# A banded attention layer: the mixes of row m-2 directly behind the scores of row m, all turns one row later, the layer's input loaded twice

## The chip, the cores and the metric

The kernel runs on one core of a Trainium2 chip. The metric is the device time of one execution in microseconds (us). All arithmetic data is float32; matrix products of the projections are made of three products of a high and a low part each.

## The reference

Two layers work on an input `x` of 128 rows x 256 tokens x 256 channels. The change touches the second layer only, which is, for each of the 128 rows by itself:

```
x2 = group_norm(x)                        # scale and shift per channel
q, k, v = split(x2 @ w_in.T + b_in)       # 4 heads of 64
scores = q @ k.T / sqrt(64)               # |i - j| <= 16 kept, else -inf
out = softmax(scores) @ v
x = x + (out @ w_out.T + b_out)
```

Its group norm is taken over all rows, so the second layer starts when the first has ended. The first layer's result `x1T` goes through memory in between.

## The kernel before

The five queues (TensorE, ScalarE, VectorE, GpSimd and the DMA queue of SyncE) each run their own hand-written list of instructions per row, `body1(m)`. A list issues in the order in which it is written; semaphores tie the lists together. `m` is the row whose scores are made in this pass, `nxt` is m+1, `last` is m-1, `far` is m+2. A pass is a software pipeline step: it holds work of several rows.

Per row TensorE does the scores (L617, 24 matmuls in the form 64x128), the projections q, k (L477) and v (L486), the final projection y (L477, input `att`), 12 matmuls each, four "turns" and the mixes. A turn transposes one head pair's probabilities through the identity matrix into the PSUM buffer `turn` (L634 to L636). The mixes multiply the turned probabilities by v (L650, form 128x64) into `mix`. There is one buffer `turn`, so a turn waits until the copy of the one before has emptied it: ScalarE copies the turns with a = 0 (L795), VectorE those with a = 1 (L1047). q and v go to `work[0]`, k and y to `work[1]`: y waits until k has been read out (`k_done`), v until q has been (`q_done`).

The other engines, per row:

- VectorE: y plus the input (L1061), eight masked minima of the scores (L1035), the reciprocals of the row sums (L1042, function `inverse`, one per group g of two heads), turn copies (L1047), the low parts of q and k (L1052, function `low`), the low part of `att` (L1077), the rounding of the normed input of row m+2 ("cast", L1082, which waits for `g_done`), its low part (L915), v plus bias (L1088).
- ScalarE: eight exponentials (L789), the high parts of q (L806) and k (L813), of `att` (L818), turn copies (L795), the edge of v (L826, L827).
- GpSimd, in this order: four normings of prob with the reciprocals of group 0 (L415, function `norms`), the normed input of row m+2 (L426, gives `g_done`), four normings of group 1.

## Time and profile before

| | us |
|---|---|
| median of 3 runs | 3655.28 |
| lowest, highest | 3653.41, 3656.13 |
| the profiled execution | 3664.15 |
| its span, first to last instruction | 3662.3 |
| first scores of the second layer, in the trace | 2366.55 |
| TensorE busy, VectorE, ScalarE, GpSimd (of the span) | 92%, 82%, 76%, 59% |

The profile comes from one execution. Its times are counted from the start of the span. The busy shares are means over both layers; for the second layer alone they are read from a stretch in its steady part. Matmuls overlap, so the time that TensorE spends on a group is read from one start to the next start, not from the durations.

### The profile page before, as it was taken

Reading aid. Unit: us, or ns where it says so; the run is one execution under the profiler, and the core shown is the slowest. Engines: PE = TensorE matmul, PEld = TensorE weight load, DVE = VectorE, ACT = ScalarE, POOL = GpSimd, SP = SyncE. Lnnn points to the kernel's source line nnn. Section 1 sums busy time; section 2 is a strip of 40 time slices with the busy share of each in tenths; the row PEclk is TensorE's granted clock in tenths of the full one; section 3 lists DMA queues with packets and bytes.
Section 4 is the critical chain, followed back from the end, with each engine's and each line's share of the span. In section 5 each row is a group of like instructions: output and inputs, shape, how many; then the busy total and the mean of one; then the engine's idle time right before and its main releaser. Section 6 shows DMA issues by size and latency. Waiting matters only on the chain.

```text
span 3662.3 us, 122873 instructions
## 1 busy us (share of the span) xinstructions
PE 3372.3 (92%) x36747; PEld 3007.4 (82%) x36747; DVE 3002.9 (82%) x10850; ACT 2776.3 (76%) x8999; POOL 2177.9 (59%) x4107
## 2 busy tenths in 40 slices
PE   4459999999999999999999999799999999999999
PEld 1148888888888888888888888699999999999998
DVE  4458988888888888888888888688888888888887
ACT  1148888988888888888888988567667677776776
POOL 0047777777777777787777777444444444444443
PEclk7569999999999999999999999899999999999999
DMA  9921111111111111111111111011111111111111
GB/s 341 349 100 54 46 49 51 44 52 45 50 52 43 52 46 48 52 43 52 46 48 50 44 52 44 30 53 52 52 52 52 52 53 54 53 52 52 52 52 47
DMA packets 189032, 238.42 MB, mean 65 GB/s; under 512 B 11824, under 2 KB 176176, under 8 KB 184752
## 3 DMA queue, kind: packets, MB, share of 16 engines
q1 hardware_dynamic: 184368, 204.17, 17.7%
q10 hardware_dynamic: 4608, 33.56, 2.5%
q8 instruction: 29, 0.48, 0.1%
q14 instruction: 27, 0.22, 0.0%
HBM read 170.57 MB, written 67.11 MB: 65 GB/s over the span
## 4 chain that ended last, share of the span: by engine, by line
PE 58%; ACT 14%; issue 11%; DMA 6%; DVE 6%; POOL 2%; DVEq 1%; SPq 1%; ACTq 1%; POOLq 0%
PE work L477 24%; ACT prob L722 7%; PE work L486 7%; PE turn L527 5%; PE score L617 5%; PE mix L650 4%; DMA x_chunk<-xT 4%; PE mix L539 3%; PE score L505 3%; DMA x_tok<-x_nat 3%; PE turn L634 3%; ACT xnT L741 2%; ACT probT L728 2%; PE turn L635 2%; PE turn L636 2%
## 5 line engine op out<-in xcount | busy, mean ns | idle before, releaser
L364 POOL TENSOR_SCALAR prob<-prob,row_inv 128x256 f32<-128x256 f32 x2048 | 1068.0, 540 | 206.1 <-DVE row_inv L932 204.9
L722 ACT ACTIVATE prob<-prob,row_min 128x256 f32<-128x256 f32 x2048 | 1028.1, 507 | 128.3 <-DVE row_min L926 123.6
L477 PE MATMUL work<-src,w 128*128 128x256 f32 x7680 | 1067.5, 288 | 10.4 <-DVE src L915 6.7
L477 PEld LDWEIGHTS work<-src,w 128*128 128x128 f32 x7680 | 951.0, 189 | 12.3 <-DVE src L915 7.4
L415 POOL TENSOR_SCALAR prob<-prob,row_inv 128x160 f32<-128x160 f32 x1024 | 391.0, 401 | 767.4 <-DVE row_inv L1042 767.4
L926 DVE CUSTOM_DVE_ANT_0 prob<-score,neg_bias 128x256 f32<-128x256 f32 x2048 | 749.5, 417 | 17.2 <-PE score L505 10.1
L527 PE MATMUL turn<-ident,prob 128*128 128x128 f32 x3072 | 484.8, 280 | 120.0 <-ACT probT L728 101.4
L789 ACT ACTIVATE prob<-prob,row_min 128x160 f32<-128x160 f32 x1024 | 431.4, 426 | 141.7 <-DVE row_min L1035 141.6
L527 PEld LDWEIGHTS turn<-ident,prob 128*128 128x128 f32 x3072 | 336.3, 141 | 233.2 <-ACT probT L728 125.6
L477 PE MATMUL work<-att,wf 128*128 128x256 f32 x3072 | 432.1, 290 | 4.4 <-DVE att L981 3.0
L486 PE MATMUL work<-w,src 128*128 128x256 f32 x3072 | 425.8, 288 | 0.0
L722 ACT ACTIVATION_READ_ACCUMULATOR prob<-prob,row_min 128x1 f32 x2048 | 397.5, 194 | 0.0
L477 PEld LDWEIGHTS work<-att,wf 128*128 128x128 f32 x3072 | 385.0, 191 | 5.1 <-DVE att L981 3.5
L486 PEld LDWEIGHTS work<-w,src 128*128 128x128 f32 x3072 | 380.6, 189 | 0.1
L728 ACT COPY probT<-turn 128x512 f32<-128x512 f32 x512 | 297.2, 580 | 76.4 <-PE turn L527 69.8
L386 POOL TENSOR_TENSOR g_tok<-x_tok,gn_row 128x512 f32<-128x512 f32 x128 | 164.5, 1285 | 189.0 <-DMA x_tok<-x_nat 181.9
L1035 DVE CUSTOM_DVE_ANT_0 prob<-score,band 128x160 f32<-128x160 f32 x1024 | 263.3, 321 | 16.5 <-issue 2.4
L505 PE MATMUL score<-kT,nqT 32*128 32x256 f32 x6144 | 251.9, 294 | 6.1 <-DVE probT L937 3.2
L539 PE MATMUL mix<-probT,v_sb 128*32 128x256 f32 x4096 | 250.3, 385 | 0.0
L505 PEld LDWEIGHTS score<-kT,nqT 32*128 32x128 f32 x6144 | 199.7, 184 | 44.3 <-DVE probT L937 14.3
L932 DVE RECIPROCAL row_inv<-row_sum 128x4 f32<-128x4 f32 x512 | 90.2, 176 | 142.3 <-ACT prob L722 135.6
L1052 DVE SCALAR_TENSOR_TENSOR kT<-work,vec_sb,kT 128x256 fp32r<-128x256 f32 x256 | 112.1, 480 | 108.8 <-ACT kT L813 108.8
(110 smaller groups left out, 6225.7 us busy)
## 6 DMA issues: line engine op xcount, KB each, us to landing
pair_chunk<-pairT ACTq DMA_DIRECT2D x32, 1024.0 KB, 8.0
x_chunk<-xT SPq DMA_DIRECT2D x32, 1024.0 KB, 8.5
x_tok<-x_nat SPq DMA_DIRECT2D x128, 256.0 KB, 3.3
x_sb<-xT SPq DMA_DIRECT2D x128, 256.0 KB, 3.4
x1T<-y_sb SPq DMA_DIRECT2D x128, 256.0 KB, 2.2
x_sb<-x1T SPq DMA_DIRECT2D x128, 256.0 KB, 2.9
outT<-y_sb SPq DMA_DIRECT2D x128, 256.0 KB, 2.2
prob<-w_d SPq DMA_DIRECT2D x1, 1024.0 KB, 8.2
```

Of the source, the lines that this page charges most:

```text
L364: pool.tensor_scalar(prob[:, h, ib], prob[:, h, ib], row_inv[:, h, ib:ib + 1], 1.0, ALU.mult, ALU.mult).then_inc(norm_done[0], 1)
L415: pool.tensor_scalar(w, w, row_inv1[:, r.base % 2, g, a, ib:ib + 1], 1.0, ALU.mult, ALU.mult).then_inc(norm_done[1], 1)
L477: ins = pe.matmul(out[:, cb], w[:, of_w, kb, cols + cb * P:cols + (cb + 1) * P], x[:, of_x, kb], start=n == 0, stop=n == len(terms) - 1)
L486: ins = pe.matmul(out[:, tb], x[:, of_x, kb, tb * P:(tb + 1) * P], w[:, of_w, kb, cols:cols + CH], start=n == 0, stop=n == len(terms) - 1)
L505: ins = pe.matmul(score[:, h, ib], nqT[q, r.base % 2, of_q, hg, ib * P:(ib + 1) * P], kT[q, r.base % 2, of_k, hg], start=n == 0, stop=n == ...
L527: ins = pe.transpose(to[:, jb * TOK + ib * P:jb * TOK + (ib + 1) * P], prob[:, h, ib, jb * P:(jb + 1) * P], ident[:])
L539: ins = pe.matmul(mix[h * D0:(h + 1) * D0, hg], v_sb[:, r.base % 2, jb, c:c + D0], probT[:, hg, h, jb], start=jb == 0, stop=jb == TB - 1, ...
L722: act.activation(prob[:, h, ib], prob[:, h, ib], ACT.Exp, bias=row_min[:, h, ib:ib + 1], scale=-1.0, accum_out=row_sum[:, h, ib:ib + 1]).t ...
L728: act.copy(probT[:, h // HPG, h % HPG].rearrange("p b t -> p (b t)"), turn[:]).then_inc(turn_done[0][0], 1)
L789: act.activation(w, w, ACT.Exp, bias=row_min1[:, m.base % 2, g, a, ib:ib + 1], scale=-1.0, accum_out=row_sum1[:, m.base % 2, g, a, ib:ib + ...
L926: dve.tensor_tensor_reduce(prob[:, h, ib], score[:, h % HPG, ib], neg_bias[:, ib, h], 1.0, 3.0e38, ALU.add, ALU.min, row_min[:, h, ib:ib + ...
L1035: dve.tensor_tensor_reduce(prob1[:, m.base % 2, g, a, ib * WIN:(ib + 1) * WIN], score[:, 2 * g + a, ib, 0:WIN], band[:, ib], 1.0, 3.0e38, ...
```

## The change

On TensorE, the mixes of row m-2 stand directly behind the scores of row m; then come the four turns of row m-1, one ahead of q, one between q and k, one between k and v, one between v and y. Before, the pass held two turns of row m-1 and two of row m, and the mixes of row m-1 stood behind k. The lists of ScalarE and VectorE follow. On VectorE the cast of row m+2 also moves ahead of the low part of k. The pipeline is one pass longer. The input is loaded twice: once for the group norm (`x_ch`, in the space of `x_tok`) and, three rows later, once for the sum with y (`x_sb`). GpSimd's list keeps its order.

```diff
+        x_ch = x_tok[:].rearrange("p r b c -> p r (b c)").rearrange("p r (c t) -> p r c t", c=CB)
...
-        v_edge = sb("v_edge", [P, 2, CH])
+        v_edge = sb("v_edge", [P, 4, CH])
...
-            rows(1, x1_v, out_v)
+            def body1(m):
+                done, far = m + -3, m + 3
+                if far.exists:
+                    wait(sp, g_done[1], far.times(1, -1))
+                    apart(sp, sp_passed)
+                    sp.dma_start(x_ch[:, far.base % 2], x1_v[:, :, far.tokens()]).then_inc(x_ch_in[far.base % 2], 16)
+                if m.exists:
+                    wait(sp, y_done[1], m.times(CB, -3 * CB))
+                    apart(sp, sp_passed)
+                    sp.dma_start(x_sb[:, m.base % XSLOTS], x1_v[:, :, m.tokens()]).then_inc(x_in[1][m.base % XSLOTS], 16)
+                if done.exists:
+                    wait(sp, y_done[1], done.times(CB, CB))
+                    apart(sp, sp_passed)
+                    sp.dma_start(out_v[:, :, done.tokens()], y_sb[:, :, done.base % 2]).then_inc(y_out[1][done.base % 2], 16)
+            over_rows(sp, 3, 3, body1)
+            for s in range(2):
+                sp.wait_ge(y_out[1][s], 16 * ROWS // 2)
...
-                    wait(pool, x_in[1][far.base % XSLOTS], far.times(16, 16, of=XSLOTS))
+                    wait(pool, x_ch_in[far.base % 2], far.times(16, 16, of=2))
                     wait(pool, src_done[1], far.times(1, -1))
                     apart(pool, pool_passed)
                     for cb in range(CB):
-                        ins = pool.tensor_scalar(g_sb[:, far.base % 2, cb], x_sb[:, far.base % XSLOTS, cb],
+                        ins = pool.tensor_scalar(g_sb[:, far.base % 2, cb], x_ch[:, far.base % 2, cb],
...
+                done = last + -1
                 if m.exists:
                     scores(m, 0)
                     scores(m, 1)
-                if last.exists:
-                    turns(last, 1, 0)
+                if done.exists:
+                    mixes(done, 0)
+                    mixes(done, 1)
+                if last.exists:
+                    turns(last, 0, 0)
                 if nxt.exists:
                     wait(pe, src_done[1], nxt.times(1, 1))
                     wait(pe, v_done[1], m.times(1, 1))
                     project(work[:, 0], w1, 0, x).then_inc(q_ps[1], 1)
                 if last.exists:
-                    turns(last, 1, 1)
-                if nxt.exists:
-                    wait(pe, y_done[1], m.times(CB, -CB))
+                    turns(last, 0, 1)
+                if nxt.exists:
+                    wait(pe, y_done[1], m.times(CB, -2 * CB))
                     project(work[:, 1], w1, CH, x).then_inc(k_ps[1], 1)
                 if last.exists:
-                    mixes(last, 0)
-                    mixes(last, 1)
-                if m.exists:
-                    turns(m, 0, 0)
+                    turns(last, 1, 0)
                 if nxt.exists:
                     wait(pe, q_done[1], nxt.times(HP, HP))
                     project_tokens(work[:, 0], w1, 2 * CH, x).then_inc(v_ps[1], 1)
-                if m.exists:
-                    turns(m, 0, 1)
-                if last.exists:
-                    wait(pe, att_done[1], last.times(1, 1))
+                if last.exists:
+                    turns(last, 1, 1)
+                if done.exists:
+                    wait(pe, att_done[1], done.times(1, 1))
                     if nxt.exists:
                         wait(pe, k_done[1], nxt.times(HP, HP))
                     else:
-                        wait(pe, y_done[1], m.times(CB, -CB))
+                        wait(pe, y_done[1], m.times(CB, -2 * CB))
                     project(work[:, 1], wf1, 0, att).then_inc(y_ps[1], 1)
-            over_rows(pe, 1, 1, body1)
+            over_rows(pe, 1, 2, body1)
...
+                done = last + -1
                 if m.exists:
                     exps(0, 0)
-                if last.exists:
-                    turn_copy(last, 1)
+                if done.exists:
+                    wait(act, mix_ps[1], done.times(HP, HP))
+                    wait(act, y_ps[1], done.times(1, 0))
+                    act.copy(att[:, HIGH], mix[:]).then_inc(att_high[1], 1)
+                if last.exists:
+                    turn_copy(last, 0)
                 if m.exists:
                     exps(0, 1)
                 if nxt.exists:
@@ -813,21 +841,18 @@
                         act.activation(kT[:, nxt.base % 2, HIGH, hp], work[:, 1, hp], ACT.Identity,
                                        bias=vec1_sb[:, 1, hp:hp + 1]).then_inc(k_high[1], 1)
                 if last.exists:
-                    wait(act, mix_ps[1], last.times(HP, HP))
-                    wait(act, y_ps[1], last.times(1, 0))
-                    act.copy(att[:, HIGH], mix[:]).then_inc(att_high[1], 1)
-                if m.exists:
-                    turn_copy(m, 0)
+                    turn_copy(last, 1)
+                if m.exists:
                     exps(1, 1)
                 if nxt.exists:
                     wait(act, v_done[1], nxt.times(1, 1))
-                    wait(act, mix_ps[1], nxt.times(HP, -HP))
-                    act.copy(v_edge[0:HALO, nxt.base % 2], v_sb[0:HALO, nxt.base % 4, 1]).then_inc(v_edge_done, 1)
-                    act.copy(v_edge[HALO:EDGE, nxt.base % 2], v_sb[P - HALO:P, nxt.base % 4, 0]).then_inc(v_edge_done, 1)
+                    wait(act, mix_ps[1], nxt.times(HP, -3 * HP))
+                    act.copy(v_edge[0:HALO, nxt.base % 4], v_sb[0:HALO, nxt.base % 4, 1]).then_inc(v_edge_done, 1)
+                    act.copy(v_edge[HALO:EDGE, nxt.base % 4], v_sb[P - HALO:P, nxt.base % 4, 0]).then_inc(v_edge_done, 1)
             act.wait_ge(prob1_clear, 1)
-            over_rows(act, 1, 1, body1)
+            over_rows(act, 1, 2, body1)
...
-                if (last + -1).exists:
-                    done = last + -1
-                    wait(dve, y_ps[1], done.times(1, 1))
-                    wait(dve, y_out[1][done.base % 2], done.times(16, 0, of=2))
+                done, old = last + -1, last + -2
+                if old.exists:
+                    wait(dve, y_ps[1], old.times(1, 1))
+                    wait(dve, y_out[1][old.base % 2], old.times(16, 0, of=2))
+                    wait(dve, x_in[1][old.base % XSLOTS], old.times(16, 16, of=XSLOTS))
+                    apart(dve, dve_passed)
                     for ob in range(CB):
-                        dve.scalar_tensor_tensor(out=y_sb[:, ob, done.base % 2], in0=work[:, 1, ob],
-                                                 scalar=y_bias[:, ob:ob + 1], in1=x_sb[:, done.base % XSLOTS, ob],
+                        dve.scalar_tensor_tensor(out=y_sb[:, ob, old.base % 2], in0=work[:, 1, ob],
+                                                 scalar=y_bias[:, ob:ob + 1], in1=x_sb[:, old.base % XSLOTS, ob],
                                                  op0=ALU.add, op1=ALU.add).then_inc(y_done[1], 1)
                 if m.exists:
                     mins(0)
                     mins(1)
+                if done.exists:
+                    wait(dve, att_high[1], done.times(1, 1))
+                    dve.tensor_tensor(att[:, LOW], mix[:], att[:, HIGH].bitcast(F32), ALU.subtract
+                                      ).then_inc(att_done[1], 1)
+                if m.exists:
                     inverse(0)
                 if last.exists:
-                    turn_copy(last, 1)
+                    turn_copy(last, 0)
                 if nxt.exists:
                     wait(dve, q_high[1], nxt.times(HP, HP))
                     low(nqT, 0, b_q1, q_done[1])
-                    wait(dve, k_high[1], nxt.times(HP, HP))
-                    low(kT, 1, vec1_sb[:, 1], k_done[1])
-                if last.exists:
-                    wait(dve, att_high[1], last.times(1, 1))
-                    dve.tensor_tensor(att[:, LOW], mix[:], att[:, HIGH].bitcast(F32), ALU.subtract
-                                      ).then_inc(att_done[1], 1)
                 if far.exists:
                     wait(dve, g_done[1], far.times(1, 1))
                     wait(dve, v_ps[1], far.times(1, -1))
                     dve.tensor_copy(src[:, far.base % 2, HIGH], g_sb[:, far.base % 2]).then_inc(src_high[1], 1)
+                if nxt.exists:
+                    wait(dve, k_high[1], nxt.times(HP, HP))
+                    low(kT, 1, vec1_sb[:, 1], k_done[1])
+                if far.exists:
                     split_low(1, far, g_sb[:, far.base % 2])
-                if m.exists:
-                    inverse(1)
                 if nxt.exists:
                     wait(dve, v_ps[1], nxt.times(1, 1))
+                    wait(dve, mix_ps[1], nxt.times(HP, -3 * HP))
                     dve.tensor_tensor(v_sb[:, nxt.base % 4], work[:, 0], bv1_sb[:].unsqueeze(1).broadcast_to([P, TB, CH]),
                                       ALU.add).then_inc(v_done[1], 1)
-                if m.exists:
-                    turn_copy(m, 0)
-            over_rows(dve, 2, 2, body1)
+                if last.exists:
+                    turn_copy(last, 1)
+                if m.exists:
+                    inverse(1)
+            over_rows(dve, 2, 3, body1)
```

TensorE's list, one row in the steady part, before. `score<-kT,nqT` are the scores, `mix` the mixes, `turn` the turns, `work<-src` q and k, `work<-w,src` v, `work<-att` y. From the scores to the turn behind the mixes:

```order
L617 MATMUL score<-kT,nqT 128x160 x24
L634 MATMUL turn<-ident,prob 128x128
L635 MATMUL turn<-ident,prob 128x128
L636 MATMUL turn<-ident_edge,prob 64x128
L477 MATMUL work<-src,w 128x256 x12
L634 MATMUL turn<-ident,prob 128x128
L635 MATMUL turn<-ident,prob 128x128
L636 MATMUL turn<-ident_edge,prob 64x128
L477 MATMUL work<-src,w 128x256 x12
L650 MATMUL mix<-probT,v_sb 64x128 x4
L650 MATMUL mix<-probT,v_edge 64x64 x2
```

The same place in TensorE's list of the change, from the scores to k:

```order
L639 MATMUL score<-kT,nqT 128x160 x24
L672 MATMUL mix<-probT,v_sb 64x128 x4
L672 MATMUL mix<-probT,v_edge 64x64 x2
L672 MATMUL mix<-probT,v_sb 64x128 x4
L672 MATMUL mix<-probT,v_edge 64x64 x2
L656 MATMUL turn<-ident,prob 128x128
L657 MATMUL turn<-ident,prob 128x128
L658 MATMUL turn<-ident_edge,prob 64x128
L499 MATMUL work<-src,w 128x256 x12
```

The mixes moved up past two turns, q and k, and stand behind the scores with nothing between them.

VectorE's list behind the last of the minima, before:

```order
L1042 RECIPROCAL row_inv<-row_sum 128x4
L1047 COPY probT<-turn 128x320
L1052 SCALAR_TENSOR_TENSOR nqT<-work,b_q,nqT 128x256 x2
L1052 SCALAR_TENSOR_TENSOR kT<-work,vec_sb,kT 128x256 x2
L1077 TENSOR_TENSOR att<-mix,att 128x512
L1082 CAST src<-g_tok 128x512
L915 TENSOR_TENSOR src<-g_tok,src 128x512
L1042 RECIPROCAL row_inv<-row_sum 128x4
L1088 TENSOR_TENSOR v_sb<-work,bv_sb 128x512
L1047 COPY probT<-turn 128x320
```

And in the change, the same place:

```order
L1096 TENSOR_TENSOR att<-mix,att 128x512
L1067 RECIPROCAL row_inv<-row_sum 128x4
L1072 COPY probT<-turn 128x320
L1077 SCALAR_TENSOR_TENSOR nqT<-work,b_q,nqT 128x256 x2
L1108 CAST src<-g_tok 128x512
L1077 SCALAR_TENSOR_TENSOR kT<-work,vec_sb,kT 128x256 x2
L940 TENSOR_TENSOR src<-g_tok,src 128x512
L1117 TENSOR_TENSOR v_sb<-work,bv_sb 128x512
L1072 COPY probT<-turn 128x320
L1067 RECIPROCAL row_inv<-row_sum 128x4
```

The low part of `att` moved ahead of the first reciprocal, the cast ahead of the low part of k, and the second reciprocal to the end of the row.

## Rows read from the trace of the kernel before

**Rows 1.** Busy time and counts per engine, granted clock, DMA share, by stretch.

```profile
400.00:1400.00 1000.00, 940.58 (x10759) 827.23 (x10758) 887.40 (x3248) 883.83 (x2755) 786.66 (x1345) 1.00 0.16 48
2800.00:3600.00 800.00, 800.00 (x8587) 765.96 (x8586) 646.39 (x2383) 560.27 (x1990) 329.05 (x796) 1.00 0.17 52
```

**Rows 2.** Chain that ended last, 2900 to 3500 us, by line.

```profile
by line: PE work L477 42.4%; PE score L617 14.7%; PE work L486 14.4%; PE mix L650 12.6%; PE turn L634 7.3%; PE turn L635 4.4%; PE turn L636 4.3%
```

**Rows 3.** Timeline of one row of layer 2, TensorE: start us, duration us.

```profile
3008.84 1.57 PE L617 MATMUL score<-kT,nqT 64*128 64x160 f32 x24
...
3010.34 0.33 PE L634 MATMUL turn<-ident,prob 128*128 128x128 f32 x1
...
3010.64 1.66 PE L477 MATMUL work<-src,w 128*128 128x256 f32 x12
...
3012.38 1.65 PE L477 MATMUL work<-src,w 128*128 128x256 f32 x12
3013.96 0.66 PE L650 MATMUL mix<-probT,v_sb 128*64 128x128 f32 x8
...
3015.22 0.33 PE L634 MATMUL turn<-ident,prob 128*128 128x128 f32 x1
...
3015.52 1.69 PE L486 MATMUL work<-w,src 128*128 128x256 f32 x12
...
3017.29 1.68 PE L477 MATMUL work<-att,wf 128*128 128x256 f32 x12
...
3018.90 1.57 PE L617 MATMUL score<-kT,nqT 64*128 64x160 f32 x24
```

**Rows 4.** The same row on ScalarE: the steps that the change puts in one chain.

```profile
3011.54 0.43 ACT L789 ACTIVATE prob<-prob,row_min 128x160 f32<-128x160 f32 x1
...
3011.96 0.42 ACT L789 ACTIVATE prob<-prob,row_min 128x160 f32<-128x160 f32 x1
...
3014.07 0.84 ACT L813 ACTIVATE kT<-work,vec_sb 128x256 fp32r<-128x256 f32 x2
...
3015.41 0.59 ACT L818 CAST att<-mix 128x512 fp32r<-128x512 f32 x1 [0.50 <-PE mix L650]
...
3015.89 0.43 ACT L795 COPY probT<-turn 128x320 f32<-128x320 f32 x1
...
3016.21 0.44 ACT L789 ACTIVATE prob<-prob,row_min 128x160 f32<-128x160 f32 x1
```

**Rows 5.** The same row on VectorE and GpSimd.

```profile
3012.51 0.18 DVE L1042 RECIPROCAL row_inv<-row_sum 128x4 f32<-128x4 f32 x1 [0.42 <-ACT prob L789]
...
3012.89 1.53 POOL L415 TENSOR_SCALAR prob<-prob,row_inv 128x160 f32<-128x160 f32 x4 [3.43 <-DVE row_inv L1042]
...
3014.40 1.09 POOL L426 TENSOR_SCALAR g_tok<-x_sb,gn_scale,gn_shift 128x256 f32<-128x256 f32 x2
3014.94 0.88 DVE L1052 SCALAR_TENSOR_TENSOR kT<-work,vec_sb,kT 128x256 fp32r<-128x256 f32 x2 [0.83 <-ACT kT L813]
...
3016.03 0.69 DVE L1077 TENSOR_TENSOR att<-mix,att 128x512 fp32r<-128x512 f32 x1 [0.21 <-ACT att L818]
...
3016.63 0.42 DVE L1082 CAST src<-g_tok 128x512 fp32r<-128x512 f32 x1
```

**Rows 6.** Chain that ended last, start of layer 2.

```profile
2356.21 1.09 POOL g_tok L426 x2
2357.39 0.73 DVE src L1082
2358.14 0.94 DVE src L915
2359.12 5.50 PE work L477 x24
```

**Rows 7.** Work on tile `g_tok`, 2355 to 2360 us: duration ns min/median/max.

```profile
L426 POOL TENSOR_SCALAR g_tok<-x_sb,gn_scale,gn_shift x4: 553/558/723, 2356.2 to 2357.8; 128x256 f32<-128x256 f32 x4
L1082 DVE CAST src<-g_tok x1: 717/717/717, 2357.4 to 2357.4; 128x512 fp32r<-128x512 f32 x1
```

More of the change, by code:

```diff
@@ L230, in conv_preact_kernel @@
         x_tok_in = [sem(f"x_tok_in{s}") for s in range(2)]
+        x_ch_in = [sem(f"x_ch_in{s}") for s in range(2)]
         gn_scaled = sem("gn_scaled")
@@ L645, in mixes @@
                     terms = [(v_sb[:, r.base % 4, jb], slice(jb * P, (jb + 1) * P), slice(jb * P, (jb + 1) * P))
-                             for jb in range(TB)] + [(v_edge[:, r.base % 2], slice(P - HALO, P + HALO), slice(TOK, TOK + EDGE))]
+                             for jb in range(TB)] + [(v_edge[:, r.base % 4], slice(P - HALO, P + HALO), slice(TOK, TOK + EDGE))]
                     for n, (v, queries, of) in enumerate(terms):
@@ L1082, in body1 @@
                     dve.tensor_copy(src[:, far.base % 2, HIGH], g_sb[:, far.base % 2]).then_inc(src_high[1], 1)
+                if nxt.exists:
+                    wait(dve, k_high[1], nxt.times(HP, HP))
+                    low(kT, 1, vec1_sb[:, 1], k_done[1])
+                if far.exists:
                     split_low(1, far, g_sb[:, far.base % 2])
+                if nxt.exists:
+                    wait(dve, v_ps[1], nxt.times(1, 1))
+                    wait(dve, mix_ps[1], nxt.times(HP, -3 * HP))
+                    dve.tensor_tensor(v_sb[:, nxt.base % 4], work[:, 0], bv1_sb[:].unsqueeze(1).broadcast_to([P, TB, CH]),
+                                      ALU.add).then_inc(v_done[1], 1)
+                if last.exists:
+                    turn_copy(last, 1)
                 if m.exists:
                     inverse(1)
-                if nxt.exists:
-                    wait(dve, v_ps[1], nxt.times(1, 1))
-                    dve.tensor_tensor(v_sb[:, nxt.base % 4], work[:, 0], bv1_sb[:].unsqueeze(1).broadcast_to([P, TB, CH]),
-                                      ALU.add).then_inc(v_done[1], 1)
-                if m.exists:
-                    turn_copy(m, 0)
-            over_rows(dve, 2, 2, body1)
+            over_rows(dve, 2, 3, body1)
 def channels(v):
```

## The prediction

> **What bounds the kernel now.** I read the busy times by stretch first, for the second layer alone. In its steady part TensorE is busy 800 us of 800 at the full granted clock (1.00, that is 2.4 GHz), VectorE 646, ScalarE 560, GpSimd 329 [rows 1]. The chain that ended last holds nothing but TensorE there [rows 2]. So the second layer takes what TensorE needs to start its matmuls, and no other engine's lateness shows. The row that I walk through lasts from 3008.84 to 3018.90 us, 10.06 us [rows 3]. From start to start it is: scores and a turn 1.80, q and a turn 1.74, k 1.58, mixes 1.26, a turn 0.30, v and a turn 1.77, y 1.61 [rows 3].
>
> **What the change takes from TensorE.** No matmul is added or removed. What changes is which forms follow each other. A turn behind the scores costs 0.30 (1.80 less 1.50, from 3008.84 to 3010.34). A turn behind k costs less: q with its turn takes 1.74, k, the same work without a turn but with mixes behind it, 1.58, so putting a turn there adds only 0.16 [rows 3]. One turn makes just this move. I price a new row from pieces: scores 1.50, mixes 1.26, a turn 0.30, q and a turn 1.74, k and a turn 1.74 (by the row of q), v and a turn 1.77, y 1.61: 9.92 us [rows 3]. That is 0.14 less per row. The one piece with no row is scores followed by mixes. Below, it is the 1.50 of scores followed by a turn, which has a change of form in it too; above, the 0.14 comes back there, and the row stays at 10.06. I take 1.50, because mixes behind scores are one change of form, as a turn behind scores is. If nothing else waited, the row would last 9.92 to 10.06 us.
>
> The Trainium skill, page TensorEngine Tiling (Array Packing), section Key Properties, says that changing the tiling mode drains TensorE. The change saves one such switch per row (scores and mixes, each in a form of its own, now stand side by side), so by this rule alone the sum would be 0.14 a row less, and the kernel faster. The trace agrees with the rule as far as the 0.14 goes; it does not show scores and mixes side by side.
>
> **What the change makes late.** Here I follow the new lists of the other engines through one pass, t = 0 at the first matmul of the scores. The mixes start at 1.50 and all that ScalarE does for group 0 now stands behind them, because its copy of `att` is second in its list, behind only two exponentials.
>
> - Mixes start 1.50. The copy of `att` starts 1.45 after the mixes start (3013.96 to 3015.41) [rows 3, 4]: t = 2.95.
> - The turn copy behind it 0.48 later, the first exponential of the pair behind that 0.32 later (3015.41, 3015.89, 3016.21) [rows 4]: 3.75.
> - Its second exponential 0.42 later (3011.54 to 3011.96), the reciprocal of group 0 0.55 after that (to 3012.51) [rows 4, 5]: 4.72. Before, the reciprocal came at t = 3.67 (3012.51 less 3008.84).
> - GpSimd's normings start 0.38 later (3012.89), its normed input of row m+2 1.51 later (3014.40) and lasts 1.09 [rows 5]: `g_done` at 7.70.
> - The cast on VectorE follows 0.09 later (2356.21 + 1.09 to 2357.39) [rows 6]: 7.79. In the new list it stands **ahead** of the low part of k. Before, GpSimd was done at t = 6.65 and the cast came at 7.79, behind the low part of k, so nobody waited.
> - Cast 0.42, low part of k 0.88 [rows 5]; neighbours on VectorE overlap by some 0.09 (the low part of `att` at 3016.03 lasts 0.69, the cast starts 3016.63) [rows 5], I take 0.08: 9.01.
> - TensorE's y writes where k lay and waits for `k_done`. A released matmul starts 0.04 after its producer's end (2358.14 + 0.94 to 2359.12) [rows 6]: y starts at 9.05 instead of 9.92 less 1.61, 8.31. A wait of 0.74 per row.
> - y to the next scores 1.61 [rows 3]: the row lasts 10.66 us.
>
> Without the cast in its way the low part of k would be in time: k starts at 1.50 + 1.26 + 0.30 + 1.74 = 4.80, ScalarE reads it 1.69 later (3012.38 to 3014.07), 0.84 long, then 0.03 and 0.88 (3014.94) [rows 3 to 5]: 8.24, and y could start at 8.28. So the cast is what decides, by its wait for GpSimd. q by the same steps: it starts at 3.06, its low part is done at 6.50, and v, which waits for it, may start at 6.54. That is without a margin, but a short wait there changes nothing at y, which starts 0.74 later anyway.
>
> Behind the waiting cast on VectorE stand the low parts of k and of the input, v plus bias, a turn copy and the second reciprocal. TensorE waits for `k_done` only: the rest is needed in the next pass. GpSimd's next normings start after the second reciprocal, about t = 10.7, and end 1.53 later, at 1.6 of the next pass; the first turn needs them at 2.76. All these have room. GpSimd cannot run ahead: in its list the normed input of row m+2 stands behind the normings of group 0 of row m, and these behind the reciprocal.
>
> The second loading adds 256 KB per row. The DMA engines are busy 0.17 of the time [rows 1] with two transfers of that size a row, so 0.25 with three. The load for row m+3 is issued when the normed input of row m+1 is done, two passes before GpSimd reads it. Cost nothing; a load that took a whole row more would still be in time. The zeroing of a `v_edge` of twice the size is one memset, once: nothing. One pass more at the end: mixes and y of the last row, 1.26 + 1.61, about 3 us [rows 3]; the first rows, which wait for nothing yet, give about 1 back.
>
> **Sum.** 10.66 less 10.06 is 0.60 a row. Of 128 rows I count 124 as steady: 74 us, and 2 for the ends: 76 us. The profiled execution, 3664.15 (span 3662.3), would become 3740. It lies 8.9 above the median of the runs shown, which I take for the difference between executions; on the median, 3655.28, the sum gives 3731 us.
>
> **Bounds.** Smaller: no gap between GpSimd and the cast and none before y (less 0.13 a row): plus 60, 3715. Larger: the 0.14 between scores and mixes comes back. It delays the whole chain, since mixes start later: plus 17, 3748. A release of TensorE as slow as that of GpSimd (0.38 less the reciprocal's 0.18, so 0.20 in place of 0.04) adds 20 [rows 5]: 3751. The likeliest case by itself has the range 3715 to 3755.
>
> A further cost is seen at the start of the layer: there the cast took 0.72 us and not 0.42, while GpSimd was still at its second pair on `g_tok` [rows 5, 7]. The Trainium skill, page SBUF — State Buffer, section SBUF: two separate sides, has VectorE and GpSimd share a pair of ports that one of them locks for a whole instruction. I don't add this 0.30: in the new steady row GpSimd has nothing to do between 7.70 and the second reciprocal, and the cast lies in that gap.
>
> **The rivals.**
>
> - **Faster: the cast is not late.** The place is GpSimd's `g_done`. If the cast started before t = 7.0, the low part of k would start when ScalarE has done its part (7.36), y would not wait, and the row would last 9.92: 0.14 x 125 less, plus 3 at the end, about 3641. For it speaks that GpSimd is busy less than half of the steady time [rows 1]; against it that its list is in order, and that my chain has to be 0.8 us shorter. It decides at a cast start of about 7.2 (y at 8.45, the row at 10.06). The rule of the Trainium skill's page on tiling, named above, is on this side. Chance 0.07. A stall of part of the size, 0.1 to 0.4 a row, gives 3670 to 3705: chance 0.05. That the stall and the gain cancel within 0.2% (7.3 us): 0.02.
> - **Much slower: a second wait joins.** VectorE has 8.1 us of work per row (646 in 800 us) [rows 1] and now waits 1.3 us at the cast; of 10.66 little is left for its other waits. Should the row's first minima slip until the copy of `att` on ScalarE comes late, or the cast hit GpSimd's work (0.30, above), I price it at 0.30: a row of 10.96, plus 114, about 3769. Chance 0.09.
> - **The granted clock falls** because TensorE now waits 7% of each row. In the first layer it idles 59 us of 1000, and the clock is 1.00 [rows 1]. Chance 0.02, price over 100 us.
>
> The likeliest case has the rest, 0.75. The range that holds the time 8 times in 10 takes it whole and reaches a little into both neighbours: 3708 to 3762. What can be told from no change is about 0.2%, 7 us. Faster 0.07, same 0.02, slower 0.91.
>
> **What the profile of the changed kernel would show.** TensorE no longer busy without gap: a wait of 0.6 to 0.9 us per row at y, released by VectorE's low part of k, and VectorE waiting some 1.3 us per row (6.50 to 7.79) at the cast for GpSimd's `g_tok`. The reciprocal of group 0 at 4.7 after the scores. From mixes to the turn behind them 1.26 as before, from scores to mixes 1.50, from k to v 1.74. The chain that ended last with ScalarE, GpSimd and VectorE in it. Granted clock 1.00. The prediction is wrong if the cast starts before 7 us in the row, if the copy of `att` is not what ScalarE's exponentials wait behind, or if rows last 9.9 us.

## The result

| | before | the change |
|---|---|---|
| median, 4 runs each | 3654.35 us | 3742.34 us |
| lowest to highest | 3650.78 to 3656.13 | 3732.01 to 3744.29 |
| ratio, 95% interval | | 1.0229 [1.0212, 1.0246] |
| span of the profiled execution | 3662.3 us | 3741.6 us |

The change makes the kernel 2.3% slower by the ratio of the runs; the medians alone are 88 us apart, 2.4%, which the interval of the ratio still holds. In the two profiled executions the second layer, from its first scores to the end, takes 85.1 us more (3741.6 - 2360.7 against 3662.3 - 2366.5 us). The first layer was 5.8 us shorter in the profile of the change; its code is the same.

The loss lies in the steady rows. Busy time by stretch, as in [rows 1] (TensorE, weight loads, VectorE, ScalarE, GpSimd, granted clock, DMA share, GB/s):

```profile
2800.00:3600.00 800.00, 760.45 (x8043) 717.72 (x8041) 595.55 (x2231) 531.56 (x1867) 308.70 (x746) 1.00 0.23 73
```

TensorE is busy 760 us of 800 and starts 8043 matmuls instead of 8587, at the same clock. Nothing runs slower; something waits. The waits of the change, 2500 to 3600 us (total us, times, longest):

```profile
...
DVE src L1108 <- POOL g_tok L448: 129.1, 103, 1.3
ACT prob L812 <- DVE row_min L1060: 121.5, 102, 1.3
PEld work L499 <- issue: 78.9, 103, 0.9
PE work L499 <- DVE kT L1077: 54.3, 103, 0.6
```

Two of them stand in no row of before: TensorE waits once a row (103 times for 103 rows) at y for the low part of k (DVE kT), and VectorE waits once a row at the cast for GpSimd. (The matmul row counts 0.5 us per row and the weight load ahead of it 0.77: the end of the matmul before is modelled. From start to start, which needs no ends, it comes out below.) The chain that ended last, 2900 to 3500 us, by line, which in [rows 2] was TensorE alone:

```profile
by line: PE work L499 15.6%; PE score L639 14.0%; issue 13.5%; PE mix L672 11.9%; POOL prob L437 10.5%; POOL g_tok L448 10.2%; ACT prob L812 8.9%; DVE kT L1077 5.2%; DVE src L1108 4.0%; DVE row_inv L1067 1.8%; ACTq L90 1.1%; ACT probT L818 
```

It now runs through all four engines. One row of it in the timeline of the change (start us, duration us), which answers to [rows 3 to 5]:

```profile
3010.14 1.57 PE L639 MATMUL score<-kT,nqT 64*128 64x160 f32 x24
...
3011.64 0.66 PE L672 MATMUL mix<-probT,v_sb 128*64 128x128 f32 x8
...
3013.09 0.59 ACT L826 CAST att<-mix 128x512 fp32r<-128x512 f32 x1 [0.51 <-PE mix L672]
...
3013.57 0.43 ACT L818 COPY probT<-turn 128x320 f32<-128x320 f32 x1
...
3013.89 0.44 ACT L812 ACTIVATE prob<-prob,row_min 128x160 f32<-128x160 f32 x1
...
3014.31 0.43 ACT L812 ACTIVATE prob<-prob,row_min 128x160 f32<-128x160 f32 x1
...
3014.86 0.18 DVE L1067 RECIPROCAL row_inv<-row_sum 128x4 f32<-128x4 f32 x1 [0.46 <-ACT prob L812]
...
3015.24 1.53 POOL L437 TENSOR_SCALAR prob<-prob,row_inv 128x160 f32<-128x160 f32 x4 [3.43 <-DVE row_inv L1067]
...
3016.76 1.09 POOL L448 TENSOR_SCALAR g_tok<-x_tok,gn_scale,gn_shift 128x256 f32<-128x256 f32 x2
...
3017.88 0.43 DVE L1108 CAST src<-g_tok 128x512 fp32r<-128x512 f32 x1 [1.24 <-POOL g_tok L448]
...
3018.23 0.87 DVE L1077 SCALAR_TENSOR_TENSOR kT<-work,vec_sb,kT 128x256 fp32r<-128x256 f32 x2
3018.25 0.27 PE L656 MATMUL turn<-ident,prob 128*128 128x128 f32 x1
...
3019.24 1.68 PE L499 MATMUL work<-att,wf 128*128 128x256 f32 x12 [0.51 <-DVE kT L1077]
```

The next scores start at 3020.85, so the row lasts 10.71 us against 10.06. Read it from the end: y starts 0.14 after the low part of k, which starts 0.35 after the cast, which starts 0.03 after GpSimd's normed input, and so on up to the mixes at 1.50 of the row. The longest gap in it between the end of one step and the start of the next is 0.20, from the reciprocal to GpSimd. The wait at y can be read from the starts alone: from the last turn to y it is 0.99 us here (3018.25 to 3019.24), and 0.24 before, where y (at 3017.29 [rows 3]) waited for nothing:

```profile
3017.05 0.27 PE L634 MATMUL turn<-ident,prob 128*128 128x128 f32 x1
```

So TensorE waits 0.75 us per row there.

### The profile page after: what moved, and what is told of

It is laid out like the page before. It is cut to its first block, busy times and chain, and to the rows that moved or that the text cites. A ratio compares the mean times of both kernels' runs of the same rounds, so it can differ in the third digit from the quotient of the medians.

```text
span 3741.6 us, 123927 instructions
## 1 busy us (share of the span) xinstructions
PE 3387.1 (91%) x36747; PEld 3005.8 (80%) x36747; DVE 2983.6 (80%) x10850; ACT 2786.7 (74%) x8999; POOL 2178.9 (58%) x4107
## 4 chain that ended last, share of the span: by engine, by line
PE 39%; ACT 17%; issue 15%; DVE 9%; POOL 9%; DMA 6%; DVEq 1%; ACTq 1%; SPq 1%; POOLq 0%
PE work L499 15%; ACT prob L745 7%; PE turn L549 5%; PE score L639 5%; PE mix L672 4%; POOL prob L437 4%; POOL g_tok L448 4%; DMA x_chunk<-xT 3%; ACT prob L812 3%; PE mix L561 3%; PE score L527 3%; DMA x_tok<-x_nat 2%; DVE kT L1077 2%; PE work L508 2%; ACT xnT L764 2%
## 5 line engine op out<-in xcount | busy, mean ns | idle before, releaser
L851 ACT COPY v_edge<-v_sb 32x256 f32<-32x256 f32 x128 | 52.0, 406 | 222.6 <-DVE v_sb L1117 222.6
```

## The experiments

Theory A is the prediction's: the cast stands ahead of the low part of k, so y waits for GpSimd; and GpSimd is late because the first reciprocal of the row stands behind the copy of `att`, which needs the mixes. Rivals: the length of VectorE's list (B), the place of the copy of `att` doesn't matter (C), the doubled load (D), the move of the cast by itself (E). F and G are rivals on GpSimd: that its idle time hides added work, and that it stays in the chain by another way. The runs e9 to e12 are on a side finding, the delay between the low part of k and y (H: two waits on one matmul cost it; I: another reason).

All runs were timed beside the kernel before on the same chip. The chips differ (the medians of before lie between 3652 and 3668 us), so the ratios are to be compared, not the times. The column "scores" is the time from the first to the last scores matmul of layer 2 in the run's own profile, less that of before. It leaves out the first layer and what follows the last scores.

| run | ratio, 95% interval | scores, us |
|---|---|---|
| the change | 1.0229 [1.0212, 1.0246] | +80.6 |
| cast behind k (e1) | 0.9987 [0.9978, 0.9996] | -11.3 |
| exponentials first (e2) | 1.0122 [1.0106, 1.0139] | +38.1 |
| normed input first (e3) | 0.9983 [0.9973, 0.9992] | -12.1 |
| before, two loads (e4) | 0.9995 [0.9987, 1.0004] | +0.1 |
| before, cast ahead (e5) | 1.0028 [1.0017, 1.0038] | +10.5 |
| GpSimd longer (e6) | 1.0420 [1.0399, 1.0442] | +148.2 |
| cast behind, GpSimd longer (e7) | 0.9995 [0.9984, 1.0005] | -11.0 |
| exponentials and reciprocal first (e8) | 0.9988 [0.9979, 0.9997] | -9.8 |
| y with one wait (e9) | 1.0226 [1.0213, 1.0239] | +70.1 |
| input first, one wait (e10) | 0.9965 [0.9952, 0.9978] | -15.1 |
| the change again (e11) | 1.0239 [1.0225, 1.0253] | +80.1 |
| one wait again (e12) | 1.0211 [1.0197, 1.0225] | +69.3 |

The rows behind that column, of the scores on TensorE, for before, the change and e1 (count, duration ns min/median/max, first and last start):

```profile
L617 PE MATMUL score<-kT,nqT x3072: 267/272/343, 2366.5 to 3645.1; 64*128 64x160 f32 x192
```

```profile
L639 PE MATMUL score<-kT,nqT x3072: 267/272/343, 2360.7 to 3719.9; 64*128 64x160 f32 x192
```

```profile
L639 PE MATMUL score<-kT,nqT x3072: 267/272/343, 2367.2 to 3634.5; 64*128 64x160 f32 x192
```

**The cast behind the low part of k (e1).**

```diff
+                if nxt.exists:
+                    wait(dve, k_high[1], nxt.times(HP, HP))
+                    low(kT, 1, vec1_sb[:, 1], k_done[1])
                 if far.exists:
                     wait(dve, g_done[1], far.times(1, 1))
                     wait(dve, v_ps[1], far.times(1, -1))
                     dve.tensor_copy(src[:, far.base % 2, HIGH], g_sb[:, far.base % 2]).then_inc(src_high[1], 1)
-                if nxt.exists:
-                    wait(dve, k_high[1], nxt.times(HP, HP))
-                    low(kT, 1, vec1_sb[:, 1], k_done[1])
```

> The changed kernel with one move on VectorE: the cast of row m+2 stands behind the low part of k again, as it did before the change. Theory A (y waits for k_done, because the cast, which waits for GpSimd's normed input, stands ahead of the low part of k): y waits no more, the row goes from 10.72 to 9.92 to 9.96 us, and the time from 3742 by some 95 us to 3647 (3638 to 3655). Rival B (the later reciprocal and VectorE's fuller list make the row long whatever stands ahead of k): most of the 0.65 us per row stays, the time is above 3700.

The ratio is 0.9987: this one place in VectorE's list is worth the whole loss, and the kernel is then slightly faster than before (0.1%; the interval ends at 0.9996). Theory B falls, since the list is as long as in the change. The waits of e1, 2600 to 3500 us:

```profile
POOL prob L437 <- DVE row_inv L1067: 529.3, 180, 3.0
...
DVE kT L1077 <- ACT kT L841: 78.9, 91, 0.9
```

VectorE waits for k itself again, not for GpSimd, and no wait of TensorE is in the list. The rows are 9.97 us on average (1267.3 less 1.3, the time from the first to the last scores matmul of one row, over 127), not quite the 9.92 of the sum. This mean is lowered by the first two rows, while the pipeline fills; in the steady part a row lasts 9.99. And y is not quite free: it still starts 0.14 us after the low part of k ends (3009.75 + 0.88 to 3010.77), as in every row of that stretch:

```profile
3009.75 0.88 DVE L1077 SCALAR_TENSOR_TENSOR kT<-work,vec_sb,kT 128x256 fp32r<-128x256 f32 x2 [0.89 <-ACT kT L841]
...
3010.77 1.67 PE L499 MATMUL work<-att,wf 128*128 128x256 f32 x12
```

The first reciprocal is as late here as in the change (4.72 of the row); it does no harm.

**The second pair of exponentials ahead of the copy of `att` on ScalarE (e2).** The exponentials `exps(0, 1)` change places with the copy of `att` and the turn copy behind it; nothing else moves.

```diff
                 if m.exists:
                     exps(0, 0)
+                if m.exists:
+                    exps(0, 1)
...
                 if last.exists:
                     turn_copy(last, 0)
-                if m.exists:
-                    exps(0, 1)
```

> The changed kernel with one move on ScalarE: the copy of att and the turn copy behind it stand behind the second pair of exponentials of group 0, so that the reciprocal needs neither the mixes nor these copies. The cast stays ahead of the low part of k. Theory A with its chain (mixes, copy of att, turn copy, exponentials, reciprocal, normings, normed input, cast): the reciprocal comes at about 3.7 us of the row instead of 4.7, GpSimd is done at about 6.7, the cast waits 0.3 us or less, the row lasts 9.92 to 10.0, the time is 3640 to 3657. Rival C (the copy of att in front of the exponentials is not what makes the chain late): 3730 to 3745.

A miss: 1.0122, rows of 10.36, about half of the loss is left. The timeline of one row of e2 shows the link that was left out:

```profile
3017.45 1.57 PE L639 MATMUL score<-kT,nqT 64*128 64x160 f32 x24
...
3020.26 0.41 ACT L812 ACTIVATE prob<-prob,row_min 128x160 f32<-128x160 f32 x1
...
3020.67 0.56 ACT L828 CAST att<-mix 128x512 fp32r<-128x512 f32 x1
...
3021.27 0.69 DVE L1096 TENSOR_TENSOR att<-mix,att 128x512 fp32r<-128x512 f32 x1 [0.56 <-ACT att L828]
...
3021.88 0.17 DVE L1067 RECIPROCAL row_inv<-row_sum 128x4 f32<-128x4 f32 x1
```

The exponentials now come first, and the last one starts at 2.81 of the row. But the reciprocal stands behind the low part of `att` on VectorE, which needs ScalarE's copy of `att`, which needs the mixes. So it came at 4.43 instead of 4.72. There are two links from the mixes to the reciprocal, one on each engine; while the first held, the second, in VectorE's list, was hidden behind it.

**Both links cut (e8).** As e2, and on VectorE:

```diff
+                if m.exists:
+                    inverse(0)
                 if done.exists:
                     wait(dve, att_high[1], done.times(1, 1))
...
-                if m.exists:
-                    inverse(0)
```

> The changed kernel with the second pair of exponentials ahead of the copy of att on ScalarE, as in the run that fell short (rows of 10.33), and in addition the first reciprocal ahead of the low part of att on VectorE. The cast stays ahead of the low part of k. In the run before, the exponentials were done at 3.3 of the row, but the reciprocal stood behind the low part of att, which waits for the copy of att, and came at 4.4. Theory A, with this second link: the reciprocal comes at 3.4, GpSimd is done at 6.35, the cast waits for nothing, the row lasts 9.95 to 10.0, the time is 0.997 to 1.000 of before. If rows stay above 10.2, the chain has a link that I don't know.

0.9988, with the cast still ahead of the low part of k. In a row of e8 whose scores start at 3014.03, the reciprocal comes at 3.29 and the cast does not wait for GpSimd, whose normed input ends at 3020.31:

```profile
3017.20 0.56 ACT L828 CAST att<-mix 128x512 fp32r<-128x512 f32 x1
3017.32 0.18 DVE L1067 RECIPROCAL row_inv<-row_sum 128x4 f32<-128x4 f32 x1
3017.79 0.69 DVE L1098 TENSOR_TENSOR att<-mix,att 128x512 fp32r<-128x512 f32 x1 [0.29 <-ACT att L828]
3019.22 1.09 POOL L448 TENSOR_SCALAR g_tok<-x_tok,gn_scale,gn_shift 128x256 f32<-128x256 f32 x2
...
3020.45 0.42 DVE L1108 CAST src<-g_tok 128x512 fp32r<-128x512 f32 x1
```

**The normed input first on GpSimd (e3).** The third place at which the chain can be cut: its step for row m+2 ahead of `norms(m, 0)` instead of behind it.

```diff
-                if m.exists:
-                    norms(m, 0)
                 if far.exists:
...
                     ins.then_inc(g_done[1], 1)
+                if m.exists:
+                    norms(m, 0)
```

> The changed kernel with one move on GpSimd: the normed input of row m+2 stands ahead of the normings of group 0 instead of behind them, so it does not need the reciprocal. Theory A: the cast finds its input ready and does not wait, the row lasts 9.92 to 9.97, the time is 3640 to 3657. Rival B (length of VectorE's list): above 3700. A rival in between (the loads come too late for an earlier normed input, or the normings, now 1.1 us later, hold up the turns): 3660 to 3700, with a wait at the turns or at GpSimd for the load.

0.9983. The loads were in time, the normings too: no wait of GpSimd for a load and none of TensorE at a turn stands in its waits, 2600 to 3500 us. Three different cuts (e1 on VectorE, e8 on ScalarE and VectorE, e3 on GpSimd) each give back the whole loss, so all of them lay in one chain. That is what theory A says, and no rival does.

**The kernel before with every row loaded twice (e4).** The second copy goes to a buffer that nobody reads.

```diff
...
+                    if n == 1 and far.exists:
+                        wait(sp, x_two_in[far.base % 2], far.times(16, 0, of=2))
+                        apart(sp, sp_passed)
+                        sp.dma_start(x_two[:, far.base % 2], of[:, :, far.tokens()]).then_inc(x_two_in[far.base % 2], 16)
...
```

> The kernel before, with every row of the second layer's input loaded a second time into a buffer that nobody reads. It prices the double load of the change by itself. Theory A: nothing, within 0.2% of 3654. Rival D (a part of the change's loss is traffic: 256 KB more per row): 10 us or more above before, with slower matmuls or later stores in the trace.

0.9995, the interval includes 1, and the scores column moves by 0.1 us. The doubled load costs nothing (D falls).

**The kernel before with only the cast moved (e5).** The same move as in the change, from behind the low part of `att` to the place ahead of the low part of k.

```diff
                     low(nqT, 0, b_q1, q_done[1])
+                if far.exists:
+                    wait(dve, g_done[1], far.times(1, 1))
+                    wait(dve, v_ps[1], far.times(1, -1))
+                    dve.tensor_copy(src[:, far.base % 2, HIGH], g_sb[:, far.base % 2]).then_inc(src_high[1], 1)
+                if nxt.exists:
                     wait(dve, k_high[1], nxt.times(HP, HP))
                     low(kT, 1, vec1_sb[:, 1], k_done[1])
...
                 if far.exists:
-                    wait(dve, g_done[1], far.times(1, 1))
-                    wait(dve, v_ps[1], far.times(1, -1))
-                    dve.tensor_copy(src[:, far.base % 2, HIGH], g_sb[:, far.base % 2]).then_inc(src_high[1], 1)
                     split_low(1, far, g_sb[:, far.base % 2])
```

> The kernel before, with only the cast of row m+2 moved ahead of the low part of k on VectorE. Theory A (the move costs only when GpSimd is late, and GpSimd is late only with the mixes ahead of the first reciprocal): the normed input is done at 6.65 of the row, the cast at 7.1, the low part of k at about 8.0, and y may start 0.15 later; before, y starts at 8.45. So nothing, within 0.2% of before. Rival E (the move by itself is the loss): 20 us or more above before.

Neither: 1.0028 [1.0017, 1.0038], some 10 us. The move alone costs an eighth of the loss, not nothing. Waits of e5, 2600 to 3500 us, and a part of one of its rows:

```profile
...
DVE src L1076 <- POOL g_tok L426: 122.7, 88, 1.6
...
PEld work L477 <- DVE att L1082: 4.5, 23, 0.3
```

```profile
3015.14 0.43 DVE L1076 CAST src<-g_tok 128x512 fp32r<-128x512 f32 x1 [1.50 <-POOL g_tok L426]
...
3015.48 0.87 DVE L1052 SCALAR_TENSOR_TENSOR kT<-work,vec_sb,kT 128x256 fp32r<-128x256 f32 x2
...
3016.26 0.68 DVE L1082 TENSOR_TENSOR att<-mix,att 128x512 fp32r<-128x512 f32 x1
...
3017.00 1.70 PE L477 MATMUL work<-att,wf 128*128 128x256 f32 x12
```

The low part of k is in time, as forecast. I had not looked at what stands behind it: the low part of `att`, which y needs as well. It now ends at 3016.94, and y starts at 3017.00. The waits list it in 23 of 88 rows, where it is long enough to count, but in each of the 108 rows between 2500 and 3600 us y starts 0.055 us after it ends. Most of the cost is in every fourth row: those last 10.26 us, the others 10.11, against 10.07 before. In every fourth row the cast starts 0.12 us after GpSimd's normed input ends and not 0.03; why, no run shows (the kernel's loop holds four rows).

**One more operation on GpSimd (e6, e7).** The edit, in the change and in e1 (the buffer `pool_extra` is read by nobody):

```diff
...
+                    for _ in range(1):
+                        pool.tensor_scalar(pool_extra[:, far.base % 2], x_ch[:, far.base % 2, 0],
+                                           gn_scale[1][:, 0:1], gn_shift[1][:, 0:1], ALU.mult, ALU.add)
```

> The changed kernel with one more operation of 256 columns on GpSimd, ahead of the normed input, into a buffer that nobody reads (some 0.55 us). Theory A: GpSimd lies in the chain of every row, so the row gets longer by the whole operation, 10.72 to 11.27, and the time by 124 x 0.55 = 68 us, to 1.041 of before. Rival F (GpSimd is idle for more than half of the row and has room for it): no more than 10 us.

> The same extra operation on GpSimd, but in the kernel with the cast behind the low part of k. Theory A: GpSimd is off the chain now, the row stays at 9.99 and the time at 0.998 to 0.999 of before, as without the operation. Rival G (GpSimd stays in a chain by another way, such as the input of the next projections): up to 68 us more.

In the change the operation costs its whole length: 148.2 less 80.6 is 67.6 us, 0.53 a row, and it takes 0.54 from its start to the start of the next one on GpSimd (3016.76 to 3017.30 in a row of e6). In e1 it costs nothing (-11.0 against -11.3 us in the scores; the two ratios, 0.9995 and 0.9987, have intervals that overlap). GpSimd is idle more than half of the time in both (busy 332 and 372 us of 800). Waits, 2600 to 3500 us, of e6:

```profile
...
PE work L503 <- DVE kT L1081: 85.5, 80, 1.1
```

and of e7:

```profile
...
DVE kT L1081 <- ACT kT L845: 77.7, 90, 0.9
```

TensorE's longest wait at y grew from 0.6 to 1.1 us in e6.

**y with one wait (e9, e12) and the best version (e10).** In the trace of the change y starts 0.15 us after the low part of k ends, while v, which waits for one semaphore, starts 0.05 after the low part of q. y waits for two, and the one written first, for `att_done`, has long been fulfilled. The edit puts one of them on the turn ahead of y:

```diff
+                if done.exists:
+                    wait(pe, att_done[1], done.times(1, 1))
                 if last.exists:
                     turns(last, 1, 1)
                 if done.exists:
-                    wait(pe, att_done[1], done.times(1, 1))
```

> The changed kernel with TensorE's wait for att_done moved from y to the turn ahead of it, where it is long fulfilled, so that y's first matmul waits for one semaphore, not for two. In the changed kernel y starts 0.15 us after the low part of k ends; v, with one wait, starts 0.05 after the low part of q. Theory H (two waits on one matmul cost the 0.09 between them): rows of 10.63 instead of 10.72, 11 us less than the changed kernel, about 1.020 of before. Rival I (the 0.15 belongs to y for another reason): no change, 1.023.

> The changed kernel once more, on the same chip and in the same rounds as the run beside it, to compare one wait and two waits at y directly. All theories: 1.022 to 1.024 of before, rows of 10.7.

> The changed kernel with the wait for att_done moved from y to the turn ahead of it, a second time. Its trace had shown y 0.05 instead of 0.15 us behind the low part of k and rows 0.08 us shorter, but its time, from another set of rounds than the changed kernel's, had shown no gain. Theory H (the trace holds for the times too): 10 us, 0.0028 of the ratio, below the changed kernel run beside it. Rival I (the profile alone shows it): the ratios differ by less than 0.001.

e9's profile showed the shorter row (+70.1 instead of +80.6 us), but its ratio did not, against the ratio of the change, which was not timed beside it. Timed side by side on one chip (e11 and e12), the two differ by 0.0028 (1.0239 and 1.0211), 11 us by the medians (3741.02 and 3729.98), as expected. The intervals touch, but all five times of e12 lie below all five of e11 (at most 3734.78 against at least 3735.77); with the profiles of e9 and e12 both 10 to 11 us shorter, I take it as real. A row of e12: the low part of k ends at 3011.35, y starts at 3011.40:

```profile
3010.48 0.87 DVE L1078 SCALAR_TENSOR_TENSOR kT<-work,vec_sb,kT 128x256 fp32r<-128x256 f32 x2
...
3011.40 1.70 PE L499 MATMUL work<-att,wf 128*128 128x256 f32 x12 [0.40 <-DVE kT L1078]
3013.03 1.57 PE L639 MATMUL score<-kT,nqT 64*128 64x160 f32 x24
```

So moving the wait is worth the 0.09. That the number of waits is the reason is not shown, and e5 speaks against it: its y has the same two waits in the same order, the one for `att_done` comes last, and y starts 0.06 after it. What sets the change apart is that the wait which comes last is the one written second. The weight load of y, just ahead of its first matmul, differs in the same way. For the change the profile names nothing that releases it ("issue"):

```profile
3019.21 1.50 PEld L499 LDWEIGHTS work<-att,wf 128*128 128x128 f32 x12 [0.75 <-issue]
```

In e12, and in e5 in the row shown above, it is released by what comes last:

```profile
3011.40 1.49 PEld L499 LDWEIGHTS work<-att,wf 128*128 128x128 f32 x12 [0.67 <-DVE kT L1078]
```

```profile
3017.00 1.49 PEld L477 LDWEIGHTS work<-att,wf 128*128 128x128 f32 x12 [0.19 <-DVE att L1082]
```

No run writes the two waits of the change in the other order, so the reason stays open.

> The kernel with the normed input first on GpSimd (rows of 9.99), with the wait for att_done moved away from y as in the run beside it. There y still started 0.04 late, by its 0.15 behind the low part of k. Theory H: y starts without a wait, rows of 9.94 to 9.96, 5 us less than with two waits, 0.997 of before or a little under. Rival I: rows stay at 9.99, 0.998.

0.9965 [0.9952, 0.9978], scores 3.0 us shorter than with two waits (e3). This is the change with the normed input first on GpSimd and one wait on y, and it beats both kernels: 3652.67 us by the median against 3664.46 of before on its chip.

## Why the prediction was right

It forecast 3731 us, 76 more than before; measured were 3742, 88 more by the medians and 85 in the profiles. No row explains the 3 us between these two. The wait at y, forecast as 0.74 us a row, was 0.75.

- **TensorE's own row.** Right in the main. Scores to mixes take 1.50 (3010.14 to 3011.64), the piece that no row had shown, so the 0.14 does not come back there. But the whole row saves less than 0.14. With y almost unhindered (e10) the rows average 9.94 us ((1263.5 - 1.3) / 127), and this mean is lowered by the first two rows; a steady row lasts 9.97, 0.10 less than before. The sum had 9.92. In one of its rows v starts at 6.58 of the row and not at 6.54, 0.05 after the low part of q ends, so the "no margin" at v cost some hundredths; y starts at 8.36 and not at 8.31:

```profile
3011.62 1.57 PE L639 MATMUL score<-kT,nqT 64*128 64x160 f32 x24
...
3017.27 0.88 DVE L1078 SCALAR_TENSOR_TENSOR nqT<-work,b_q,nqT 128x256 fp32r<-128x256 f32 x2
...
3018.20 1.70 PE L508 MATMUL work<-w,src 128*128 128x256 f32 x12
...
3019.98 1.68 PE L499 MATMUL work<-att,wf 128*128 128x256 f32 x12
...
3021.59 1.12 PE L639 MATMUL score<-kT,nqT 64*128 64x160 f32 x16
```

- **The chain and its decider.** Right, link by link: copy of `att` at 2.95 of the row, reciprocal at 4.72, GpSimd done at 7.71, cast at 7.74, y at 9.10; forecast were 2.95, 4.72, 7.70, 7.79 and 9.05. e1 shows that the cast's place is needed, e3 that the normings ahead of the normed input are, e8 that the copies ahead of the exponentials together with VectorE's own link are, and e6 that the chain has no slack. The copy of `att` and the turn copy behind it were only moved together.
- **What was mis-sized: the step "a released matmul starts 0.04 after its producer's end".** It took 0.14 to 0.15 at y, with the two waits as they are written there (e12: 0.05 with one of them moved). The gap between GpSimd and the cast was smaller than I took (0.03, not 0.09). The two errors have opposite signs, so it is partly luck that the row came out at 10.71 against 10.66: 6 us over 124 rows. In every fourth row that gap is 0.12 instead of 0.03, and the row 0.09 longer, so that the mean steady row is 10.72. The bound for a slow release, 0.20, had held it.
- **The ends.** Counted row by row, 124 rows are 81.4 us longer (0.657 each, where I had 0.60, 74 us). The first two rows, while the pipeline fills, give 1.6 back, where I had 1; the last row is 0.9 longer, and what follows the last scores grew from 17.2 to 21.7 us: 5.4 together, where I had 3. That makes the 85 us.
- **Cost nothing.** The doubled load: right (e4). VectorE's fuller list: right (e1).
- **"So the cast is what decides".** Right for the change. That "nobody waited" before holds too, but e5's forecast drew too much from it: with little room at y, the same cast also costs 10 us in the kernel before, over the low part of `att`.
- **"Its copy of `att` is second in its list".** Right as a cause, but not the only one: VectorE's list held the same link once more, and e2, built on the first alone, got back half.

## What to carry to other kernels

When a list of instructions is reordered to serve one engine, walk the other lists from the moved work to the next thing that the busy engine waits for, across engines; here the mixes moved up by 3.6 us and pulled a reciprocal, an idle GpSimd and a cast behind them. An engine that is idle for more than half of the time can be on the path in every row; whether it is, one added operation on it tells (0.53 us a row, or nothing). An instruction that waits for a slow neighbour does not belong ahead of one that the bounding engine waits for, and when one link of a chain is cut, look in each list for a second that does the same.

## What was unexpected in the hardware

- A matmul with two waits, of which the one written second came last, started 0.147 us after it; with the other wait moved to an earlier instruction it started 0.054 after. The same kernel, the same producer; 11 us over the run. With the wait written first coming last (e5) it was 0.055, with both waits in place. The reason is open.
- Scores and mixes, groups of matmuls of the forms 64x128 and 128x64, cost no more to change between than scores and a turn (128x128): 1.50 us from the start of the scores in both cases.
- The hand-over from GpSimd to a waiting cast on VectorE took 0.03 us in three rows of four and 0.12 in the fourth (77 and 25 rows of the change). The reason is open.
